# A decoder layer on one core: rotary halves exchanged by DMA, three-pass attention scores, top-4 by match and replace

## Chip, cores and metric

One core of one Trainium2 chip runs the whole layer in one launch. The metric is the device time of a launch in microseconds (us): lower is better. The median of three runs of the kernel before is 417.92 us (417.89 to 418.08).

## What is computed

Four sequences (`B`=4) of 256 tokens with 256 channels pass through one layer: self-attention, cross-attention and a block-sparse feed-forward network, each followed by a residual sum and a layer norm. Cut to what the change touches:

```python
# self-attention: 16 query heads, 2 key/value heads of 128
qkv = hidden_states @ Wqkv
x1, x2 = (x[..., :D // 2], x[..., D // 2:])            # rotary embedding of q and k
out = jnp.concatenate([x1 * cos - x2 * sin, x1 * sin + x2 * cos], axis=-1)
logits = jnp.einsum('bqhd,bkhd->bhqk', xq, xk) * SCALE
logits = SOFTCAP * jnp.tanh(logits / SOFTCAP)          # then causal mask, softmax, @ xv, @ Wo
# feed-forward router: the 4 most probable of 16 blocks of 64 hidden units
prob = jax.nn.softmax(xf @ Wr.T + br, axis=-1)
_, idx = jax.lax.top_k(prob, TOP_K)
mask = mask.at[jnp.arange(n)[:, None], idx].set(1.0)
h = jax.nn.gelu(h, approximate=False) * mask[:, :, None]
```

## The kernel before

Work is cut into operations `(kind, b, i, t)`: a kind, a sequence b, an index i (a head pair, a quad of heads, a half of the network) and, for the parts that go by token tile, the tile t of 128 tokens. Each engine runs its own share of every operation, in one common order, `plan`. `plan` is built from the string `ORDER`: each letter takes the next operation of one stream (`r` rotary projections, `s` scores, `m` probabilities times values and the output projection, `c` context, `x` and `y` cross-attention of tile 0 and 1, `n` and `o` the network of tile 0 and 1). So an engine whose next instruction waits holds up all that stands behind it in `plan`, on that engine alone; engines meet through semaphores. SP, the queue that issues nearly all DMAs, walks the same `plan`. PSUM has seven rotating banks (`claim`), and an eighth for the sum of the output projection (`acc`).

The parts that the change touches:

- `rot(b, i)`: PE projects one pair of heads (i=0 is the keys), 24 matmuls of 256 columns in three passes over parts of the operands (high times high, high times low, low times high: `three_pass`, L438). DVE's `rope` multiplies the bank by cosine (L928) and, each half of the partitions apart, the exchanged halves by sine (L931, L932) into `rope_t`. POOL's `rotate` adds the two (L1223) into `q_T` or `k_T`. `q_T` has four pair slots.
- `near(b, j)` and `far(b, i)`: PE multiplies keys and queries in plain fp32, 512 columns in one matmul (L469, L477). ACT applies tanh and exp (L773, L775), POOL the causal selection (L1241). `mix` on PE (L492, L495) then needs what POOL selected.
- `turn(b, j)`: PE transposes a pair's output; ACT takes it out of PSUM twice, rounded into `a_hi` and as it is into `a_flat`; POOL subtracts (L1234, `a_lo`); `proj` on PE (L525) needs `a_lo`.
- `wo`: ACT rounds (L791) and POOL takes the rest (L1229) of a weight slot, for the first sequence alone; later ones reload the parts (`wo_s<-wo_parts`).
- `route(b, t)`: DVE turns 16 probabilities into a mask of 4 by comparing each with each: L1125, L1126, L1130, L1132, L1134, then L1137. `turn_m`, the masked half of `hidden` and `ffn` on PE wait for it.
- `turn_q`: ACT copies transposed queries into `qS`, two quads of heads deep for each tile.

Of the kernel before, what the change touches and what calls it, by code (L numbers as in the profile page):

```python
# [65 lines left out]
def rotate_ops(b):  # L66
# [8 lines left out]
    return [(kind, b, i, 0) for kind, i in ops]  # L75

# [46 lines left out]
def network_ops(b, t):  # L123
# [12 lines left out]
    "rrrrrrrrrmmsrssrrmmsmrmssmrmmrrmmmsscmmmsmmmmmmccmmsssmmmcccmmmmrrmmmmccmmmrmmrrmsssmccmmmrmmsssmmmyrmmmx"  # L136
    "rsmssxyrmmmxmsmymrmmxsmysxxmmmmyrrymymmmxxxxysyryrmmrmyxyyxxxxyyxyxmmxyyxxymmmxmssxrrxyyxysxmymyyssxmmmmy"
    "xxccmmmsrsrnsmmmmsxyrcmcccmmymmsmsyxmrmmmxnmmmmmxxmnymrrnnyxxxxyyrxxxxmyxyyxxxxmyyxmmoxyyyxroyyxyymssxyym"
    "xosryyxroxysymysmmxmmsyccnoxymycomcomyccxsymnssrymxmymxxymyrxsxxmyxxyxxyyxyyyoymmxxyxxyxyymxyxxnyyxsxxsym"
    "yyxmmmmoxynmmmmmycmmcmmmmnxyccccooxnxyynxyxxyoyoxyyyyxyyxyyonxyyyxxxxyxxxyxyxxyyxxnyxyxyoxooyynnxnxnnnooo"  # L140
    "nnnoonoo")


# [24 lines left out]
PER = {"x_hi": 1, "x_lo": 1, "roped": 3 * (PAIRS + 1), "rotated": PAIRS + 1, "values": 1,  # L168
# [9 lines left out]
def build_decoder(nc, x, xT, ctxT, mask, wqkv, wo, wkvT, xwq, xwo, xbias, wrT, br, w1T, w2T,  # L178
# [10 lines left out]
    with ExitStack() as ctx:  # L189
# [42 lines left out]
        a_flat = sb("a_flat", [2, 2, T])  # L232
# [1083 lines left out]
```

## Time and profile before

| | |
|---|---|
| median of three runs | 417.92 us (417.89 to 418.08) |
| profiled execution, its own time | 418.27 us |
| its span, first to last instruction | 416.5 us |
| PE busy | 383.6 us, 92% |
| DVE busy | 345.8 us, 83% |
| ACT busy | 248.2 us, 60% |
| POOL busy | 151.3 us, 36% |
| granted TensorE clock | 0.999 of full speed |

Busy times are those of the page. A busy PE is one with a matmul in its pipeline, and PE's instructions overlap: a 256-column matmul is shown with 0.28 us though the next one starts after 0.12 us. Costs of PE are therefore read from distances between starts.

### The profile page before, as it was taken

What the parts mean: (1) busy time and instruction counts of PE and PEld (TensorE: products, weight loads), DVE (VectorE), ACT (ScalarE), POOL (GpSimd) and SP (SyncE); (2) the same over time, 40 slices, a digit from 0 to 9 for tenths busy, and PEclk for the clock granted to TensorE, in tenths of its full rate; (3) what the DMA queues carried; (4) which work ended last, traced back from release to release, by engine and by line L of the source; (5) the groups of instructions that cost most, each with busy time, mean ns of one, the idle gap of its engine ahead of it and who ended that gap; (6) DMA issues with size and microseconds to landing.
All of it is one profiled execution on the core that took longest, in us unless ns stands there. A gap on an engine that the chain in (4) does not pass through costs nothing.

```text
span 416.5 us, 9192 instructions
## 1 busy us (share of the span) xinstructions
PE 383.6 (92%) x3144; PEld 327.9 (79%) x3144; DVE 345.8 (83%) x967; ACT 248.2 (60%) x528; POOL 151.3 (36%) x174
## 2 busy tenths in 40 slices
PE   2889999999999999999999999999889989889895
PEld 2868779887799877788998686978768977668784
DVE  4999987589989679889997998888798887888753
ACT  5266543545777775365689665389974247984230
POOL 7488636745544233455331133143113221000101
PEclk9999999999999999999999999999999999999999
DMA  6993342511311230213303000121103000000000
GB/s 213 334 344 127 124 144 89 182 48 51 102 50 53 84 121 2 76 58 105 121 1 102 2 27 27 39 65 51 52 27 103 2 0 14 15 2 0 14 15 25
DMA packets 16814, 31.36 MB, mean 75 GB/s; under 512 B 1665, under 2 KB 10753, under 8 KB 16769
## 3 DMA queue, kind: packets, MB, share of 16 engines
q1 hardware_dynamic: 15952, 29.98, 21.8%
q10 hardware_dynamic: 816, 0.79, 0.7%
q8 instruction: 27, 0.44, 0.4%
q14 instruction: 19, 0.15, 0.1%
HBM read 25.52 MB, written 5.24 MB: 74 GB/s over the span
## 4 chain that ended last, share of the span: by engine, by line
PE 48%; DVE 30%; issue 9%; ACT 6%; POOL 3%; DMA 3%; SPq 0%; DVEq 0%; POOLq 0%; ACTq 0%
PE bank L438 10%; PE acc L525 7%; PE bank L611 4%; PE bank L492 4%; PE bank L663 3%; PE bank L469 3%; PE bank L600 3%; ACT xs L817 2%; PE bank L506 2%; PE bank L623 2%; DMA xs<-in_wo 2%; PE bank L477 2%; DVE rope_t L932 2%; DVE rope_t L931 2%; PE bank L678 2%
## 5 line engine op out<-in xcount | busy, mean ns | idle before, releaser
L1223 POOL TENSOR_TENSOR q_T<-q_T,rope_t 128x512 f32<-128x512 f32 x32 | 43.0, 1345 | 45.0 <-DVE rope_t L932 45.0
L817 ACT ACTIVATE xs<-xs,xneg 128x256 f32<-128x256 f32 x128 | 54.5, 502 | 6.6 <-DVE xneg L1069 6.4
L1234 POOL TENSOR_TENSOR a_lo<-a_flat,a_hi 128x512 fp32r<-128x512 f32 x32 | 41.9, 1310 | 38.6 <-ACT a_flat L738 38.6
L438 PE MATMUL bank<-x_hi,wqkv_hi 128*128 128x256 f32 x144 | 45.6, 317 | 8.8 <-DVE wqkv_lo L904 8.8
L1252 POOL TENSOR_TENSOR rstd<-var_eps,half 128x1 f32<-128x1 f32 x24 | 13.2, 552 | 108.0 <-DVE var_eps L956 108.0
L525 PE MATMUL acc<-wo_s,a_hi 128*128 128x256 f32 x256 | 50.4, 295 | 0.9 <-POOL a_lo L1234 0.9
L1069 DVE CUSTOM_DVE_ANT_0 xs<-bank,mask_s 128x256 f32<-128x256 f32 x128 | 46.0, 418 | 0.6 <-PE bank L600 0.6
L492 PE MATMUL bank<-v_s,p_near 128*128 128x129 f32 x256 | 42.5, 278 | 1.2 <-POOL p_far L1241 0.8
L525 PEld LDWEIGHTS acc<-wo_s,a_hi 128*128 128x128 f32 x256 | 39.5, 189 | 3.8 <-issue 2.1
L492 PEld LDWEIGHTS bank<-v_s,p_near 128*128 128x128 f32 x256 | 35.8, 191 | 8.4 <-issue 6.6
L438 PE MATMUL bank<-x_lo,wqkv_hi 128*128 128x256 f32 x144 | 41.7, 289 | 0.0
L438 PE MATMUL bank<-x_hi,wqkv_lo 128*128 128x256 f32 x144 | 41.6, 289 | 0.0
L611 PE MATMUL bank<-ident_s,xs 128*128 128x128 f32 x256 | 36.2, 277 | 1.2 <-ACT xs L817 0.4
L438 PEld LDWEIGHTS bank<-x_hi,wqkv_hi 128*128 128x128 f32 x144 | 28.5, 198 | 10.5 <-issue 10.0
L525 PE MATMUL acc<-wo_s,a_lo 128*128 128x256 f32 x128 | 35.9, 280 | 0.0
L773 ACT ACTIVATE p_near<-bank 128x512 f32<-128x512 f32 x32 | 19.1, 596 | 26.7 <-PE bank L469 26.5
L738 ACT CAST a_hi<-bank 128x512 fp32r<-128x512 f32 x32 | 18.9, 591 | 24.3 <-PE bank L506 23.7
L611 PEld LDWEIGHTS bank<-ident_s,xs 128*128 128x128 f32 x256 | 28.4, 141 | 6.3 <-issue 3.4
L469 PE MATMUL bank<-q_T,k_T 128*128 128x512 f32 x64 | 32.3, 598 | 0.1
L663 PE MATMUL bank<-z_T,w_s 128*128 128x128 f32 x256 | 31.8, 277 | 0.5 <-DVE stage L1144 0.5
L663 PEld LDWEIGHTS bank<-z_T,w_s 128*128 128x128 f32 x256 | 30.0, 192 | 0.8 <-DVE stage L1144 0.7
L678 PE MATMUL bank<-w_s,stage 128*128 128x256 f32 x128 | 29.2, 381 | 0.5 <-DVE stage L1144 0.5
(150 smaller groups left out, 976.2 us busy)
## 6 DMA issues: line engine op xcount, KB each, us to landing
wo_s<-wo_parts SPq DMA_DIRECT2D x24, 512.0 KB, 3.3
wo_parts<-wo_s SPq DMA_DIRECT2D x8, 512.0 KB, 2.9
stage<-in_wqkv SPq DMA_DIRECT2D x5, 512.0 KB, 4.3
xs<-in_wo SPq DMA_DIRECT2D x8, 256.0 KB, 4.3
y<-in_x SPq DMA_DIRECT2D x4, 256.0 KB, 2.7
ctx_s<-in_ctxT SPq DMA_DIRECT2D x4, 256.0 KB, 4.7
mask_s<-in_mask SPq DMA_DIRECT2D x4, 256.0 KB, 2.7
w_s<-in_w1T SPq DMA_DIRECT2D x1, 1024.0 KB, 11.3
```

Of the source, the lines that this page charges most:

```text
L438: ins = mm(ps, lhs[i], rhs[j], start=(k == 0 and n == 0), stop=(last and n == 2))
L469: mm(ps[:, :], k_T[:, j // 4, 0:P], q_T[:, j % 4].rearrange("p h q -> p (h q)"), start=True, stop=True).then_inc(filled, 1)
L492: ins = mm(o, p_near[:, j % NEAR, m, t * P:(t + 1) * P], v_s[:, 0, j // 4, :], start=True, stop=(t == 0))
L525: ins = mm(acc[:, t, :], a[x], wo_s[:, slot, w, m, :], start=(j == 0 and t == 0 and m == 0 and p == 0), stop=(j == PAIRS - 1 and m == 1 an ...
L611: ins = transpose(ps[:, m2 * T + k * P:m2 * T + (k + 1) * P], xs[:, t, m, m2, k * P:(k + 1) * P], ident_s[:])
L663: ins = mm(ps[:, m * P:(m + 1) * P], w1_s[:, k, (n * part + m) * P:(n * part + m + 1) * P], z_T[:, t, k, :], start=(k == 0), stop=(k == CK ...
L678: ins = mm(ps[:, 0:C], g_T[:, t, n, :], w2_s[:, n, :], start=(n == 0), stop=(n == HT - 1))
L773: activation(dst, bank(kind, b, i)[:], ACT.Tanh, scale=SCALE / SOFTCAP).then_inc(sig["capped", 0], 1)
L817: activation(xs[:, t, m, m2, :], xs[:, t, m, m2, :], ACT.Exp, bias=xneg[:, t, m, m2:m2 + 1], scale=-1.0)\
L1069: do(v.tensor_tensor_reduce(out=xs[:, t, m, m2, :], in0=bank("xscore", b, g, t, m)[:, m2 * T:(m2 + 1) * T], in1=mask_s[:, t, :], scale=-1. ...
L1223: g.tensor_tensor(dst, dst, rope_t[:, n % 2], ALU.add).then_inc(sig["rotated", 0], 1)
L1234: g.tensor_tensor(a_lo[:, j % 2], a_flat[:, j % 2], a_hi[:, j % 2].bitcast(F32), ALU.subtract)\
```

## The change

Five edits. The rotary result is rounded on ACT into a high part (`q_hi`, `k_hi`), and POOL takes the rest (`q_lo`, `k_lo`), a new operation `round` with the letter `q` in `ORDER`; the scores become three passes of 512 columns. From the second sequence on DVE multiplies by sine over all 128 partitions, and two DMAs exchange the halves into `rope_s`; POOL adds after they have landed. The router takes DVE's eight largest values, marks four of them by `match_replace`, and compares. `a_flat` and `qS` have one buffer where they had two, `ones` lies inside `xs`, and the DMA scratch is smaller. `ORDER` is a new string, of 569 letters after 533.

```diff
-    "rrrrrrrrrmmsrssrrmmsmrmssmrmmrrmmmsscmmmsmmmmmmccmmsssmmmcccmmmmrrmmmmccmmmrmmrrmsssmccmmmrmmsssmmmyrmmmx"
+    "rrrrrqrqmmrrqrmqrsssqrrsmmqmrssmmmmqsrmmmmmqssrmmmmcrmqmmsmccmmmmssrrmcmmmqqmcrmcmmmmsqmmrrmmmsqqmccmsrrm"
...
-        a_flat = sb("a_flat", [2, 2, T])
+        a_flat = sb("a_flat", [2, T])
-        qS = sb("qS", [TT, 2, 2, 2, P], F32R)
+        qS = sb("qS", [TT, 2, 2, P], F32R)
...
+            def swap_halves(b, i):
+
+                n = b * (PAIRS + 1) + i
+                lower, upper = slice(0, HD // 2), slice(HD // 2, HD)
+                if n >= 2:
+                    sp.wait_ge(sig["rotated", 0], n - 1)
+                wait_for(sp, "roped", b, 3 * i)
+                for dst, src in ((lower, upper), (upper, lower)):
+                    sp.dma_start(rope_s[dst, n % 2], rope_t[src, n % 2]).then_inc(swapped[n % 2], 16)
...
             def near(b, j):
...
-                wait_for(pe, "rotated", b, j + 1)
-                mm(ps[:, :], k_T[:, j // 4, 0:P], q_T[:, j % 4].rearrange("p h q -> p (h q)"),
-                   start=True, stop=True).then_inc(filled, 1)
+                wait_for(pe, "q_lo", b, j + 1)
+                three_pass(ps[:, :], [a[:, j // 4, 0:P] for a in (k_hi, k_lo)],
+                           [a[:, j % 4].rearrange("p h q -> p (h q)") for a in (q_hi, q_lo)], 0, True).then_inc(filled, 1)
...
+            def rounding(b, i):
+
+                if i == 0:
+                    wait_filled(act, "far", b - 1, QUADS - 1)
+                else:
+                    j = i - 1
+                    wait_filled(act, "far", *((b, (j - 4) // 2) if j >= 4 else (b - 1, (j + PAIRS - 4) // 2)))
+                wait_for(act, "rotated", b, i)
+                copy(rotary(i)[0], rope_c[:, (b * (PAIRS + 1) + i) % 2]).then_inc(sig["q_hi", 0], 1)
...
+                evacuate(a_hi[:, j % 2].rearrange("p h q -> p (h q)"), bank("turn", b, j)[:], "turn", b, j, 0, "attn_T")
+                if j or b:
+                    wait_for(act, "attn_lo", *divmod(b * PAIRS + j - 1, PAIRS))
+                evacuate(a_flat[:].rearrange("p h q -> p (h q)"), bank("turn", b, j)[:], "turn", b, j, 0, "attn_T")
...
-                wait_filled(act, "xscore", *((b, g - 2) if g >= 2 else (b - 1, g + QUADS - 2)), t, 1)
+                wait_filled(act, "xscore", *((b, g - 1) if g else (b - 1, QUADS - 1)), t, 1)
...
                 if n >= 2:
-                    dve.wait_ge(sig["rotated", 0], n - 1)
...
+                    dve.wait_ge(sig["q_lo", 0], n - 1)
+                dst = rope_c[:, n % 2]
...
+                if b:
+                    if n >= PAIRS + 3:
+                        dve.wait_ge(swapped[n % 2], 32 * swaps_before(n))
+                    v.tensor_tensor(rope_t[:, n % 2], ps, s, ALU.mult).then_inc(sig["roped", 0], 1)
+                    v.tensor_tensor(dst, ps, c, ALU.mult).then_inc(sig["roped", 0], 2)
+                    return
...
-                do(v.tensor_tensor(above[:, t], other, own, ALU.is_gt))
-                do(v.tensor_tensor(equal[:, t], other, own, ALU.is_equal))
+                do(v.max(best[:, t, 8 - TOPK:16 - TOPK], prob[:, t, :]))
...
-                do(v.tensor_tensor(equal[:, t], equal[:, t], before_s[:], ALU.mult))
-                done()
-                do(v.tensor_tensor(above[:, t], above[:, t], equal[:, t], ALU.add))
-                done()
-                do(v.tensor_reduce(rank[:, t, :], above[:, t], AX_X, ALU.add))
+                do(v.match_replace(marked[:, t, :], best[:, t, 0:8], prob[:, t, :], -1.0))
...
                 wait_for(pool, "roped", b, 3 * i + 2)
-                g.tensor_tensor(dst, dst, rope_t[:, n % 2], ALU.add).then_inc(sig["rotated", 0], 1)
+                if b:
+                    pool.wait_ge(swapped[n % 2], 32 * (swaps_before(n) + 1))
+                g.tensor_tensor(dst, dst, (rope_s if b else rope_t)[:, n % 2], ALU.add).then_inc(sig["rotated", 0], 1)
+
+            def rounding(b, i):
+
+                hi, lo = rotary(i)
+                wait_for(pool, "q_hi", b, i)
+                g.tensor_tensor(lo, rope_c[:, (b * (PAIRS + 1) + i) % 2], hi.bitcast(F32), ALU.subtract).then_inc(sig["q_lo", 0], 1)
```

What the new string does is seen in each engine's order. POOL's queue at the start of the first sequence, right behind the constants, was (`q_T<-q_T,rope_t` is a `rotate`, `wo_s` the rest of an output weight, `p_near` and `p_far` causal selections):

```order
L1223 TENSOR_TENSOR k_T<-k_T,rope_t 128x512
L1223 TENSOR_TENSOR q_T<-q_T,rope_t 128x512 x3
L1229 TENSOR_TENSOR wo_s<-xs,wo_s 128x512
L1241 AFFINE_SELECT p_near<-p_near 128x2x128
L1223 TENSOR_TENSOR q_T<-q_T,rope_t 128x512
L1241 AFFINE_SELECT p_near<-p_near 128x2x128
L1241 AFFINE_SELECT p_far<-p_far 128x512
L1223 TENSOR_TENSOR q_T<-q_T,rope_t 128x512
```

And now (`rope_c` is the rotary sum, `k_lo` and `q_lo` the new rests):

```order
L1256 TENSOR_TENSOR rope_c<-rope_c,rope_t 128x512 x2
L1262 TENSOR_TENSOR k_lo<-rope_c,k_hi 128x512
L1262 TENSOR_TENSOR q_lo<-rope_c,q_hi 128x512
L1268 TENSOR_TENSOR wo_s<-xs,wo_s 128x512
L1256 TENSOR_TENSOR rope_c<-rope_c,rope_t 128x512 x2
L1262 TENSOR_TENSOR q_lo<-rope_c,q_hi 128x512
L1268 TENSOR_TENSOR wo_s<-xs,wo_s 128x512
L1262 TENSOR_TENSOR q_lo<-rope_c,q_hi 128x512
L1256 TENSOR_TENSOR rope_c<-rope_c,rope_t 128x512
L1280 AFFINE_SELECT p_near<-p_near 128x2x128 x2
L1280 AFFINE_SELECT p_far<-p_far 128x512
L1262 TENSOR_TENSOR q_lo<-rope_c,q_hi 128x512
```

Each rotation now has a second POOL instruction some places behind it, and the third and fourth rotation have moved behind the first output weight.

DVE's queue in a router of the last sequence was:

```order
L1119 RECIPROCAL r_rec<-r_sum 128x1
L1121 TENSOR_SCALAR prob<-prob,r_rec 128x16
L1125 TENSOR_TENSOR above<-prob 128x256
L1126 TENSOR_TENSOR equal<-prob 128x256
L1130 TENSOR_TENSOR equal<-equal,before_s 128x256
L1132 TENSOR_TENSOR above<-above,equal 128x256
L1134 TENSOR_REDUCE rank<-above 128x16
L1137 TENSOR_SCALAR keep<-rank 128x16
```

And now:

```order
L1158 RECIPROCAL r_rec<-r_sum 128x1
L1160 TENSOR_SCALAR prob<-prob,r_rec 128x16
L1162 MAX best<-prob 128x8
L1166 MATCH_REPLACE marked<-best,prob 128x16
L1169 TENSOR_SCALAR keep<-marked 128x16
```

Two instructions on 16 values stand where five stood on 256.

SP's queue from the last stores of the first sequence to the second sequence's first reload of output weights (`L391` is `swap_halves`, two DMAs a rotation) is now:

```order
L380 DMA wo_parts<-wo_s 128x1024
L391 DMA rope_s<-rope_t 64x512 x4
L367 DMA xs<-in_wo 128x2x256
L380 DMA wo_parts<-wo_s 128x1024
L391 DMA rope_s<-rope_t 64x512 x2
L367 DMA xs<-in_wo 128x2x256
L395 DMA ctx_s<-in_ctxT 128x2x256
L380 DMA wo_parts<-wo_s 128x1024
L375 DMA wo_s<-wo_parts 128x1024
L391 DMA rope_s<-rope_t 64x512 x4
```

Before, the same stretch had the same loads and stores without the rows of L391: 54 such DMAs are new in the whole program.

## Rows read from the trace of the kernel before

**Rows 1.** Window, length, busy PE, PEld, DVE, ACT, POOL, granted clock, DMA share, GB/s

```profile
12.00:66.00 54.00, 50.49 (x340) 41.65 (x339) 50.31 (x92) 27.77 (x50) 34.07 (x33) 1.00 0.59 201
66.00:120.00 54.00, 52.36 (x383) 45.46 (x382) 42.78 (x103) 31.74 (x63) 32.45 (x35) 1.00 0.30 98
120.00:200.00 80.00, 77.66 (x672) 66.89 (x672) 68.33 (x190) 48.95 (x107) 33.40 (x37) 1.00 0.21 67
200.00:300.00 100.00, 96.73 (x855) 82.57 (x854) 88.41 (x281) 74.87 (x166) 28.33 (x33) 1.00 0.16 49
300.00:392.00 92.00, 82.88 (x752) 69.92 (x753) 77.15 (x258) 54.54 (x128) 13.97 (x18) 1.00 0.06 19
392.00:417.00 25.00, 18.85 (x132) 16.79 (x130) 12.36 (x39) 5.03 (x10) 1.65 (x3) 0.98 0.07 22
```

**Rows 2.** What PE waited for: us in total, times, longest

```profile
PE bank L438 <- DVE wqkv_lo L904: 8.8, 2, 7.4
PE bank L623 <- DVE xp_T L1078: 4.3, 6, 0.9
```

**Rows 3.** The chain that ended last, by engine (the page)

```profile
PE 48%; DVE 30%; issue 9%; ACT 6%; POOL 3%; DMA 3%; SPq 0%; DVEq 0%; POOLq 0%; ACTq 0%
```

**Rows 4.** PE in order of time: start, us shown, instruction

```profile
18.59 0.28 PE L438 MATMUL bank<-wqkv_lo,x_hi 128*128 128x256 f32 x1
18.71 0.28 PE L438 MATMUL bank<-wqkv_hi,x_lo 128*128 128x256 f32 x1
...
21.10 1.02 PE L469 MATMUL bank<-q_T,k_T 128*128 128x512 f32 x2
21.96 1.02 PE L477 MATMUL bank<-q_T,k_T 128*128 128x512 f32 x2
```

**Rows 5.** DVE's groups by form: busy us and mean ns, idle before

```profile
L931 DVE TENSOR_TENSOR rope_t<-bank,sin_s 64x512 f32<-64x512 f32 x36 | 25.0, 693 | 1.1
L932 DVE TENSOR_TENSOR rope_t<-bank,sin_s 64x512 f32<-64x512 f32 x36 | 24.6, 684 | 1.1
L928 DVE TENSOR_TENSOR q_T<-bank,cos_s 128x512 f32<-128x512 f32 x32 | 21.9, 686 | 5.1 <-PE bank L438 4.8
L1121 DVE TENSOR_SCALAR prob<-prob,r_rec 128x16 f32<-128x16 f32 x8 | 2.0, 255 | 0.3
```

**Rows 6.** The chain in the last stretch: start, us, what

```profile
398.44 0.42 DVE above L1125
...
399.89 0.43 DVE rank L1134
```

**Rows 7.** Groups of POOL and ACT by form, as in rows 5

```profile
L1223 POOL TENSOR_TENSOR q_T<-q_T,rope_t 128x512 f32<-128x512 f32 x32 | 43.0, 1345 | 45.0 <-DVE rope_t L932 45.0
L1234 POOL TENSOR_TENSOR a_lo<-a_flat,a_hi 128x512 fp32r<-128x512 f32 x32 | 41.9, 1310 | 38.6 <-ACT a_flat L738 38.6
L1241 POOL TENSOR_SCALAR_AFFINE_SELECT p_near<-p_near 128x256 f32<-128x256 f32 x32 | 14.2, 447 | 30.5 <-ACT p_near L775 30.4
L1229 POOL TENSOR_TENSOR wo_s<-xs,wo_s 128x512 fp32r<-128x512 f32 x8 | 11.2, 1404 | 9.4 <-ACT wo_s L791 9.4
L1241 POOL TENSOR_SCALAR_AFFINE_SELECT p_far<-p_far 128x512 f32<-128x512 f32 x16 | 10.4, 648 | 10.9 <-ACT p_far L775 10.9
L751 ACT CAST x_hi<-xT_s 128x512 fp32r<-128x512 f32 x4 | 2.5, 616 | 2.0 <-DMA xT_s<-in_xT 1.6 <-PE bank L438 0.4
```

**Rows 8.** POOL in order of time, idle before in brackets

```profile
12.63 1.29 POOL L1223 TENSOR_TENSOR k_T<-k_T,rope_t 128x512 f32<-128x512 f32 x1 [4.42 <-DVE rope_t L932]
15.12 1.79 POOL L1223 TENSOR_TENSOR q_T<-q_T,rope_t 128x512 f32<-128x512 f32 x1 [1.19 <-DVE rope_t L932]
```

**Rows 9.** DMAs: SP's issue of a 128 KB store, its landing; a larger reload

```profile
L420 SPq DMA_DIRECT2D out_y<-stage x8: 332/335/357, 264.3 to 414.4; - x8
DMA to landing us min/median/max: 1.7/1.7/2.0
wo_s<-wo_parts SPq DMA_DIRECT2D x24, 512.0 KB, 3.3
```

**Rows 10.** One DVE line: ns min/median/max of ten

```profile
L904 DVE TENSOR_TENSOR wqkv_lo<-stage,wqkv_hi x10: 677/1100/1780, 5.8 to 28.9; 128x512 fp32r<-128x512 f32 x10
```

More of the change, by code:

```diff
@@ L75, in rotate_ops, with round_ops @@
     return [(kind, b, i, 0) for kind, i in ops]
+def round_ops(b):
+    return [("round", b, i, 0) for i in range(PAIRS + 1)]
 def score_ops(b):
@@ L163, in make_plan @@
     return plan
[L168 removed]
+PER = {"x_hi": 1, "x_lo": 1, "roped": 3 * (PAIRS + 1), "rotated": PAIRS + 1, "q_hi": PAIRS + 1, "q_lo": PAIRS + 1, "values": 1,
        "capped": PAIRS + QUADS, "expd": PAIRS + QUADS, "causal": PAIRS + QUADS, "attn_rec": NH,
@@ L222, in build_decoder @@
         x_hi, x_lo = sb("x_hi", [CK, T], F32R), sb("x_lo", [CK, T], F32R)
-        rope_t = sb("rope_t", [2, 2, T])
-        q_T = sb("q_T", [4, 2, T])
-        k_T = sb("k_T", [NKV, T])
+        rope_t, rope_c, rope_s = (sb(name, [2, 2, T]) for name in ("rope_t", "rope_c", "rope_s"))
+        q_hi, q_lo = sb("q_hi", [4, 2, T], F32R), sb("q_lo", [4, 2, T], F32R)
+        k_hi, k_lo = sb("k_hi", [NKV, T], F32R), sb("k_lo", [NKV, T], F32R)
         v_s = sb("v_s", [TT, NKV, HD + 1])
@@ L287, in build_decoder @@
         wo_hi, wo_lo = sem("wo_hi"), sem("wo_lo")
+        swapped = [sem(f"swapped{i}") for i in range(2)]
         piece_hi, piece_lo = sem("piece_hi"), sem("piece_lo")
@@ L303, in bank, with rotary, swaps_before @@
             return banks[where[kind, b, i, t, k] % NBANK]
+        def rotary(i):
+            pair = (k_hi[:], k_lo[:]) if i == 0 else (q_hi[:, (i - 1) % 4], q_lo[:, (i - 1) % 4])
+            return pair
+        def swaps_before(n):
+            return len(range(PAIRS + 1 + (n - PAIRS - 1) % 2, n, 2))
         def wait_filled(eng, kind, b, i=0, t=0, k=0):
@@ L405, in _ @@
                 both = all((kind, b, i, n) in done for n in range(TT))
-                if kind == "quant_w" and i == 1:
+                if kind == "rot" and b:
+                    swap_halves(b, i)
+                elif kind == "quant_w" and i == 1:
                     load_tokens(1)
@@ L542, in turn_w @@
                 for o in range(CK):
-                    ins = mm(ps[:, o * P:(o + 1) * P], ones[:], q_tmp[:, o, 0:P], start=True, stop=True)
+                    ins = mm(ps[:, o * P:(o + 1) * P], ones, q_tmp[:, o, 0:P], start=True, stop=True)
                 ins.then_inc(filled, 1)
@@ L845, in _ @@
                     val(b)
+                elif kind == "round":
+                    rounding(b, i)
                 elif kind in ("near", "far"):
@@ L1233, in rest_attn @@
                 wait_for(pool, "attn_T", b, 2 * j + 1)
-                g.tensor_tensor(a_lo[:, j % 2], a_flat[:, j % 2], a_hi[:, j % 2].bitcast(F32), ALU.subtract)\
+                g.tensor_tensor(a_lo[:, j % 2], a_flat[:], a_hi[:, j % 2].bitcast(F32), ALU.subtract)\
                     .then_inc(sig["attn_lo", 0], 1)
@@ L1258, in _ @@
                     rotate(b, i)
+                elif kind == "round":
+                    rounding(b, i)
                 elif kind == "wo":
```

62 lines of the change are left out of this document (24 added, 38 removed).

## Prediction

> **What bounds the kernel now.** I read the busy times in stretches first, to see which engine is full where; then what PE waited for; then the chain that ended last. In the stretches [rows 1] PE is busy 50.5 of 54 us, 52.4 of 54, 77.7 of 80, 96.7 of 100: from 12 to 300 us it stands idle for 10.8 us of 288, under 4%. After 300 us it is looser: 9.1 us idle of 92, and 5.7 us between 392 us and the end at 416.5. No wait of PE is large but the start, where it waits for the first weights to be split (8.8 us in two waits, 7.4 of them before its first matmul); the next in the list, for DVE's `xp_T`, is 4.3 us in six pieces [rows 2]. The chain goes 48% through PE and 30% through DVE [rows 3], so DVE, busy 50.3 of 54 us in the first stretch and 88.4 of 100 in the fourth [rows 1], is a near second. POOL is full nowhere: at most 34.1 of 54 us, in the first stretch [rows 1]. So I count first what PE's own work loses, and then look where other engines' waits could reach PE.
>
> **Scores on PE.** A score matmul of 512 columns in fp32 is two records, and from the start of one to the start of the next score passes 21.96 − 21.10 = 0.86 us [rows 4]. A pass of the three-pass kind on 256 columns passes in 18.71 − 18.59 = 0.12 us [rows 4]. No such pass of 512 columns is in this trace. From above it is two of 256, 0.24, so three are 0.72 us. From below, the fp32 score taken as four passes makes 0.215 a pass, and three are 0.645 us. I take the middle, 0.68, since a wider matmul pays its fixed part once: 0.18 us less for each of 48 scores (12 in each of four sequences), 8.6 us; the bounds are 48 × 0.14 = 6.7 and 48 × 0.215 = 10.3. This is PE's own time in stretches in which it is over 95% busy, so it should come off the end.
>
> The Trainium skill (FP8 and Floating Point Precision, "TensorE Precision Notes") says that true FP32 takes four passes through the array; the two records of 0.43 us fit this as two passes each, and by the page alone a score would fall to three quarters, 0.645 us, which is the bound from below and 10.3 us in all.
>
> **Rotary products on DVE.** In sequences 1 to 3, 27 rotations lose one of their three products, which take 0.69, 0.68 and 0.69 us [rows 5] whether on 64 or 128 partitions: 27 × 0.69 = 18.6 us of DVE. In the first sequence nothing is saved.
>
> **Router on DVE.** From the start of L1125 to the end of L1134 pass 399.89 + 0.43 − 398.44 = 1.88 us [rows 6]. For the two new instructions the nearest row on 16 values is a product of 0.255 us [rows 5]; two such, with a short wait between them, are 0.55. From below they could not be less than nothing, which adds 0.55 a router. From above, each could take 0.43, as L1134 does on 256 values [rows 6]: 0.9. I take 0.55, so 1.3 us less for each of eight routers, 10.6 us of DVE. DVE's load falls by 29 us in all. In the last stretch two routers lie in the chain one behind the other, so up to 2.7 us could come off; PE's own 18.9 of 24.5 us there [rows 1] leave 5.7 us of idle, part of it behind the last matmul, so I take 2.0.
>
> DVE's relief elsewhere: between 300 and 392 us PE idles 9.1 us [rows 1], in part for DVE. Four routers fall there, which gives DVE back 5.3 us. I take a quarter of that as seen by PE, 1.3 us; the bounds are 0 and, were DVE behind all of it, 5.3.
>
> **Rounding on ACT and POOL.** 36 rotations each gain a cast of 0.62 us on ACT (22 us, from 248 of 416 us) and a subtraction on POOL like L1234, 1.31 us (47 us, from 151) [rows 7]. Both engines have the room in the sum; the question is the queue. In the first sequence a rotation waits for the `q_lo` of the last but one. I followed POOL's new order from 12.6 us [rows 8] with 1.3 us for each sum and rest, 0.45 and 0.65 for selections, 1.4 for an output weight [rows 7]: the second `rotate` starts at 15.1 [rows 8], the two rests end at about 19.5, the first weight at 20.9, rotations three and four at about 25, and the third rest at about 26.4. PE starts at 7.4 [rows 2]; three rotations and the values (each 24 passes of 0.12, 2.9 us) are done at 18.9 and two more rotations at 24.6; it does the first score and stands before the second at 25.3: a wait of 1.1 us. Against that, the values now stand ahead of the third rotation and cover PE's other wait for split weights, 8.8 − 7.4 = 1.4 us [rows 2]. From there POOL is nearly full up to 65 us: 34.1 us of work in that stretch before [rows 1], and eleven rests of 1.31 more, 48 of 54 us. Small stalls of PE in front of `mix`, `near` and `proj` will come of this; net I book +1.5 us for the start (bounds 0 and 5).
>
> **The exchange by DMA.** SP takes 0.34 us to issue a DMA, and 128 KB land after 1.7 us [rows 9]. The two of a rotation land about 0.34 + 0.34 + 1.7 = 2.4 us after `rope_t`, that is 0.69 + 2.4 = 3.1 us after DVE began, where the third product ended at 2.1: POOL's sum starts 1.0 us later. Behind a reload of 512 KB, which alone takes 3.3 us [rows 9], it may be 2 more. While POOL stands at the sum, the rests for `proj`, the selections for `mix` and the powers that the layer norms wait for stand behind it. The cover is PE's own rotation, 2.9 us, and that POOL idled 45 us for the same release already [rows 7]. A rotation and its rounding now pass in 0.69 + 2.4 + 1.3 + 0.6 + 1.3 = 6.3 us with two in flight, 3.2 us each, against PE's 2.9, and only where rotations stand back to back. I book +2.0 us for 27 rotations (bounds 0 and 8). SP waits at an exchange for `rope_t`; the reloads behind it come in the same order as before, with three slots of lead, and I book nothing; without that lead a reload that lands late would cost `proj` its 3.3 us.
>
> **The rest, at nothing.** `turn_q` with one `qS` waits for a score that stands ahead of it on PE, so it is over when the transposed queries arrive. The second copy into `a_flat` waits for POOL's last rest; where POOL is punctual, a `proj` of twelve passes, 1.4 us, lies between. Uncovered it would be up to 1.3 us each. ACT loads a table of functions ten times where it was twelve; ACT is not full, and this covers part of the new casts. `ones` and the scratch move nothing that an engine executes.
>
> **Sum.** 416.5 − 8.6 − 2.0 − 1.3 + 1.5 + 2.0 = 408.1 of span. The execution's own time is 1.8 us above its span and 0.35 above the median, so 408.1 + 1.4 = 409.5 us on the scale of the medians, 8.4 below 417.92, or 2.0%.
>
> **Rivals.**
> *DVE was the holder.* DVE is 79 to 93% busy in the stretches up to 392 us and 30% of the chain [rows 1, 3]. If most of PE's small waits were its doing, its 29 us of relief would also take half of the 20 us that PE idles between 12 and 392: 409.5 − 8 = 401.5. Against it: PE's listed waits for DVE are few [rows 2].
> *POOL becomes the bound at the start.* If each of the first nine `q_lo` reached PE half a microsecond late beyond what I booked, and `proj` likewise, the start costs its upper bound of 5 us and 2 more: 415. For it, 48 of 54 us of POOL's time filled; against it, PE itself was busy 50.5 of the same 54 [rows 1], more than POOL will be.
> *POOL stands before the exchange, and PE behind it: slower.* If the exchange's 1.0 us is seen by PE in each of 27 rotations at 0.4 us or more, on top of the bound of 5 at the start, this is 10.8 + 5 − 3.5 already booked = 12.3 more: 421.8. It decides from about 8.4/27 = 0.31 us a rotation beyond what I booked. For it: POOL executes in plan order, and its queue also carries the layer norms' powers; SP's queue stands in front of exchanges behind 512 KB reloads. Against it: POOL is busy a third of the time after 66 us [rows 1].
> *POOL and DVE in each other's way.* L904, two SBUF inputs, took 0.68 us at best and 1.10 in the median [rows 10], and POOL's sum beside it took 1.79 where it takes 1.29 [rows 8]. Each of 36 new subtractions that meets such a DVE instruction so costs 0.5 us on either side; if half meet, 9 us of each engine, which the 29 us of relief swallow. All 36, each seen by PE for a third, would be 6 us: 415.5. The Trainium skill (SBUF — State Buffer, "SBUF: two separate sides") has DVE with two SBUF inputs and a reading GpSimd exclude each other for a whole instruction. By it a meeting would cost up to 1.3 us, 36 × 1.3 = 47 us of DVE in the worst case, more than the relief; the row's 0.5 us is far less than that.
> *The transfer is no faster.* That the rotary edit brings nothing in time is already my forecast: its relief is not on PE.
>
> **Chances.** My own case, 405 to 413: 0.60. DVE's relief counts, below 405: 0.13. POOL at the start or the two engines in each other's way, 413 to 417: 0.13. The slower case, over 418: 0.11. The rest, within 0.2% of 417.92, which is about what this kernel's measurement can tell: 0.03. Faster by over 0.2%: 0.84; within 0.2%: 0.04; slower: 0.12. The range that leaves out 2 in 10 runs from 402 to 417.
>
> **What the next profile would show.** Scores: three records a score, 0.645 to 0.72 us from first to next; otherwise the first term is mis-sized. DVE busy near 317 us; far above, the engines are in each other's way (L904's new line tells it). PE's busy time 375 us. PE's waits between 20 and 60 us for `q_lo`, `p_near` or `a_lo` of at most 3 us together. POOL's waits for `rope_s` DMAs, with PE waiting for POOL in sequences 1 to 3 hardly at all. If PE's idle time between 66 and 300 us rises from 7.2 to over 15, the prediction is wrong by the exchange.

## The result: 3.3% slower

The changed kernel takes 431.31 us in the median of four runs (430.09 to 432.67), where the kernel before, run beside it on the same chip, takes 417.9. The ratio is 1.0325, 95% interval 1.029 to 1.0359: 13.4 us slower. The forecast was 409.5 us, and faster; it lies 22 us off, and the range missed as well. Ratios are of undisturbed executions alone: one of a_warm's four (632.2 us, mean granted clock 0.56) and one of the kernel beside it (484.06 us, 0.76) are left out. The profiled execution took 430.29 us, its span is 428.5.

The page after: busy times, the share of PE's clock in tenths by slice, and the shares of the chain that ended last.

```profile
span 428.5 us, 9480 instructions
PE 383.0 (89%) x3192; PEld 340.7 (79%) x3192; DVE 325.2 (76%) x924; ACT 263.1 (61%) x562; POOL 196.1 (46%) x209
...
PEclk9989969999999999999999998999999999999999
...
PE 49%; DVE 18%; POOL 9%; issue 9%; ACT 6%; DMA 6%; SPq 2%; POOLq 0%; DVEq 0%; ACTq 0%
```

DVE's share of the chain fell from 30% to 18% [rows 3], as its relief would let one expect. But POOL, the DMAs and SP's queue now hold 17% together, where POOL and DMAs held 6%, and the end came later. The same stretches as in [rows 1]:

```profile
core 0: us, PE busy (x) PEld busy (x) DVE busy (x) ACT busy (x) POOL busy (x), PEclk, DMA share, GB/s
12.00:66.00 54.00, 44.01 (x295) 40.19 (x294) 43.67 (x78) 32.36 (x58) 44.90 (x41) 0.91 0.55 189
66.00:120.00 54.00, 50.64 (x374) 45.08 (x372) 34.81 (x77) 28.24 (x53) 40.40 (x40) 1.00 0.45 132
120.00:200.00 80.00, 74.47 (x656) 66.26 (x657) 62.80 (x179) 55.27 (x123) 43.45 (x43) 1.00 0.33 93
200.00:300.00 100.00, 93.86 (x799) 84.03 (x799) 83.62 (x243) 66.91 (x145) 45.32 (x47) 0.98 0.27 75
```

From 12 to 300 us PE stands idle for 25.0 us (288 − 263.0), where it was 10.8. The first stretch gives 6.5 of these 14.2 us, at a mean clock of 0.91; the later ones give the rest. POOL is busy 44.9 of 54 us in the first. The waits after, PE's own and the largest of POOL and ACT around the rotary:

```profile
engine line waited for: us in total, times, longest us
POOL rope_c L1256 <- DMA rope_s<-rope_t: 53.6, 19, 6.5
ACT q_hi L786 <- POOL rope_c L1256: 28.8, 14, 6.2
POOL a_lo L1273 <- ACT a_flat L763: 26.3, 15, 4.7
...
PE bank L463 <- DVE wqkv_lo L943: 8.9, 2, 7.4
PE bank L463 <- POOL q_lo L1262: 5.6, 2, 4.9
PE bank L636 <- ACT xs L854: 3.3, 4, 1.9
```

Only 5.6 us of PE's waits bear the name of `q_lo`. The remaining loss has no large wait of its own: it is spread over many small gaps. So the list alone doesn't explain the result. The timeline of PE at the first scores, and of POOL beside it:

```profile
19.84 0.40 PE L463 MATMUL bank<-q_hi,k_hi 128*128 128x512 f32 x1
20.08 0.40 PE L463 MATMUL bank<-q_lo,k_hi 128*128 128x512 f32 x1
20.31 0.40 PE L463 MATMUL bank<-q_hi,k_lo 128*128 128x512 f32 x1
25.58 0.77 PE L463 MATMUL bank<-q_hi,k_hi 128*128 128x512 f32 x1 [4.87 <-POOL q_lo L1262]
26.14 0.63 PE L463 MATMUL bank<-q_lo,k_hi 128*128 128x512 f32 x1
26.57 0.63 PE L463 MATMUL bank<-q_hi,k_lo 128*128 128x512 f32 x1
26.99 0.63 PE L463 MATMUL bank<-q_hi,k_hi 128*128 128x512 f32 x1
```

```profile
20.56 1.27 POOL L1256 TENSOR_TENSOR rope_c<-rope_c,rope_t 128x512 f32<-128x512 f32 x1
22.49 1.27 POOL L1256 TENSOR_TENSOR rope_c<-rope_c,rope_t 128x512 f32<-128x512 f32 x1 [0.65 <-DVE rope_t L971]
23.71 1.73 POOL L1262 TENSOR_TENSOR q_lo<-rope_c,q_hi 128x512 fp32r<-128x512 f32 x1
25.40 1.73 POOL L1268 TENSOR_TENSOR wo_s<-xs,wo_s 128x512 fp32r<-128x512 f32 x1
```

A pass of 512 columns passes in 20.31 − 20.08 = 0.23 us. The second score needs the rest that POOL begins at 23.71, behind two sums, and PE stands 4.87 us for it. After that wait a pass takes 26.57 − 26.14 = 0.43 us, nearly twice as long: the clock has gone from 2.4 to 1.2 GHz, and stays there 3.4 us.

POOL's costliest groups, and SP's rows at exchanges between 80 and 102 us:

```profile
L1262 POOL TENSOR_TENSOR q_lo<-rope_c,q_hi 128x512 fp32r<-128x512 f32 x32 | 43.4, 1366 | 4.5 <-ACT q_hi L786 4.5
L1256 POOL TENSOR_TENSOR rope_c<-rope_c,rope_s 128x512 f32<-128x512 f32 x27 | 35.0, 1297 | 53.9 <-DMA rope_s<-rope_t 53.6
```

```profile
L391 SPq DMA_DIRECT2D rope_s<-rope_t x8: 462/568/597, 84.0 to 99.6; - x8
...
DMA to landing us min/median/max: 2.2/2.8/5.3
```

From the start of DVE's first rotary product to the start of POOL's sum now pass 4.5, 3.7 and 4.1 us on average in sequences 1, 2 and 3, where it was 2.2 to 2.8. From the end of a rotation on PE until its operand is ready pass 12.5, 12.5 and 10.7 us; before, it was 5.3, 4.4 and 4.4. In sequence 0, where nothing is exchanged, 5.4 became 8.8. These are means that I worked out from the starts and ends of the instructions of each rotation. For sequence 1 the same count gives 7.1 us without the rounding (a_fp32 below) and 9.1 with the rounding but without POOL's rests (a_norest).

### The profile page after: what moved, and what is told of

Its sections match the earlier page's. It is cut to its first block, busy times and chain, and to the rows that moved or that the text cites. A ratio compares the mean times of both kernels' runs of the same rounds, so it can differ in the third digit from the quotient of the medians.

```text
span 428.5 us, 9480 instructions
## 1 busy us (share of the span) xinstructions
PE 383.0 (89%) x3192; PEld 340.7 (79%) x3192; DVE 325.2 (76%) x924; ACT 263.1 (61%) x562; POOL 196.1 (46%) x209
## 3 DMA queue, kind: packets, MB, share of 16 engines
q1 hardware_dynamic: 20272, 37.06, 28.5%
## 4 chain that ended last, share of the span: by engine, by line
PE 49%; DVE 18%; POOL 9%; issue 9%; ACT 6%; DMA 6%; SPq 2%; POOLq 0%; DVEq 0%; ACTq 0%
PE bank L463 12%; PE bank L636 5%; PE acc L550 5%; PE bank L703 5%; PE bank L688 5%; DMA rope_s<-rope_t 4%; POOL rope_c L1256 3%; PE bank L517 3%; PE bank L625 3%; PE bank L648 2%; ACT xs L854 2%; POOL q_lo L1262 2%; PE bank L531 2%; PE bank L520 2%; POOL rstd L1291 1%
## 5 line engine op out<-in xcount | busy, mean ns | idle before, releaser
L1256 POOL TENSOR_TENSOR rope_c<-rope_c,rope_s 128x512 f32<-128x512 f32 x27 | 35.0, 1297 | 53.9 <-DMA rope_s<-rope_t 53.6
L463 PE MATMUL bank<-x_hi,wqkv_hi 128*128 128x256 f32 x144 | 43.2, 300 | 9.0 <-DVE wqkv_lo L943 8.9
L550 PE MATMUL acc<-wo_s,a_hi 128*128 128x256 f32 x256 | 48.7, 289 | 1.5 <-POOL a_lo L1273 1.3
L1262 POOL TENSOR_TENSOR q_lo<-rope_c,q_hi 128x512 fp32r<-128x512 f32 x32 | 43.4, 1366 | 4.5 <-ACT q_hi L786 4.5
L636 PE MATMUL bank<-ident_s,xs 128*128 128x128 f32 x256 | 37.2, 282 | 3.5 <-ACT xs L854 3.3
L786 ACT CAST q_hi<-rope_c 128x512 fp32r<-128x512 f32 x32 | 19.6, 620 | 30.7 <-POOL rope_c L1256 28.8
L463 PEld LDWEIGHTS bank<-x_hi,wqkv_hi 128*128 128x128 f32 x144 | 28.2, 196 | 10.3 <-issue 9.9
L1117 DVE COPY xp_T<-bank 128x512 f32<-128x512 f32 x32 | 22.0, 687 | 11.8 <-PE bank L636 11.7
L763 ACT CAST a_hi<-bank 128x512 fp32r<-128x512 f32 x32 | 18.7, 584 | 19.5 <-PE bank L531 19.1
```

The lines of the kernel that those rows point to most:

```text
L463: ins = mm(ps, lhs[i], rhs[j], start=(k == 0 and n == 0), stop=(last and n == 2))
L550: ins = mm(acc[:, t, :], a[x], wo_s[:, slot, w, m, :], start=(j == 0 and t == 0 and m == 0 and p == 0), stop=(j == PAIRS - 1 and m == 1 an ...
L636: ins = transpose(ps[:, m2 * T + k * P:m2 * T + (k + 1) * P], xs[:, t, m, m2, k * P:(k + 1) * P], ident_s[:])
L1117: v.tensor_copy(xp_T[:, t, 1].rearrange("p m k q -> p (m k q)"), bank("turn_p", b, i, t)[:])\
L1256: g.tensor_tensor(dst, dst, (rope_s if b else rope_t)[:, n % 2], ALU.add).then_inc(sig["rotated", 0], 1)
L1262: g.tensor_tensor(lo, rope_c[:, (b * (PAIRS + 1) + i) % 2], hi.bitcast(F32), ALU.subtract).then_inc(sig["q_lo", 0], 1)
```

## The experiments

Two letters stand in the names. Runs a_… have the new `ORDER` (a_start a rearranged one), runs bo_… the changed code with the old `ORDER`, into which the letter `q` is put three operations behind each rotation; where there is no rounding, `q` does nothing. b_router is the kernel before with one edit. The kernel before took 417.6 to 418.1 us in each call.

### One part at a time

**b_router**: the kernel before with the new router alone.

```diff
-                do(v.tensor_tensor(above[:, t], other, own, ALU.is_gt))
-                do(v.tensor_tensor(equal[:, t], other, own, ALU.is_equal))
...
+                do(v.max(best[:, t, 8 - TOPK:16 - TOPK], prob[:, t, :]))
...
```

> The kernel before with the new router alone (eight largest, match and replace), its own order and all else. From the trace the two new instructions take 0.43 us where five took 1.88: about 1.4 us less for each of eight routers. If two of them are seen in the tail, as predicted, 415 (2 to 3 us less than 417.9); if PE hides them, 417 to 418.

Measured: 414.10 us, ratio 0.9911 (0.9894 to 0.9927): 3.95 us off the 418.05 beside it. My terms for the router, 2.0 + 1.3, were close in sum.

**a_noswap, a_fp32, a_neither**: the changed kernel without the exchange, without the rounding, without both.

```diff
-                if b:
...
-                    v.tensor_tensor(rope_t[:, n % 2], ps, s, ALU.mult).then_inc(sig["roped", 0], 1)
-                    v.tensor_tensor(dst, ps, c, ALU.mult).then_inc(sig["roped", 0], 2)
-                    return
...
-                three_pass(ps[:, :], [a[:, j // 4, 0:P] for a in (k_hi, k_lo)],
...
+                mm(ps[:, :], k_T[:, j // 4, 0:P], q_T[:, j % 4].rearrange("p h q -> p (h q)"),
```

> The changed kernel without the exchange: in all four sequences DVE makes three products and POOL adds as soon as they are there, no DMA of rope_s. All else, the order too, as changed (431.3 us). Theory S (the loss is made at the start, where POOL's queue of sums, rests and weights keeps the second score waiting and PE's clock then falls): nothing changes before 66 us, and the time stays within 2 us of 431. Theory X (the loss comes from POOL standing 53.6 us before the landing of exchanges in sequences 1 to 3): about 7 us come back, 424. Theory D (DVE is the real second bound): 27 third products, 18.6 us, come back onto DVE, and the time rises above 433.

> The changed kernel with scores in plain fp32: no rounding on ACT, no rest on POOL, one fp32 matmul a score; the exchange, the router, the buffers and the order (round operations left out) as changed. Theory S: the wait of 4.9 us before the second score and both falls of the clock before 66 us go; scores cost 48 x 0.16 = 7.7 us more; 431.3 - 11 + 7.7 = about 428. Theory X: nothing comes back, 431 to 439.

> The changed kernel with neither the exchange nor the three-pass scores: what is left of the change is the new order (round operations left out), the router and the single buffers. If the order by itself suits the old work, 413 to 418, near the kernel before less the router's gain. If the order is part of the loss, over 420. With the other two runs this gives the exchange's cost without rounding (a_fp32 less this) and the rounding's without exchange (a_noswap less this).

Measured: a_noswap 440.58 us, 1.0547 (1.0523 to 1.0572); a_fp32 419.94, 1.004 (1.0022 to 1.0057); a_neither 430.22, 1.0297 (1.0281 to 1.0313). So in the new order the exchange saves 9.3 us with rounding (440.6 to 431.3) and 10.3 without (430.2 to 419.9), and the rounding costs 11.4 us with exchange and 10.4 without. The exchange, which I had booked as a loss, is the only part besides the router that helps. And with neither, the kernel is 12 us slower than before: something that the forecast had no term for. Of the expectations, the third of a_noswap (DVE is a second bound) and the second of a_neither (the order is part of the loss) came true; both of a_fp32 missed, the nearer by 8 us.

**bo_neither, bo_swap, bo_round, bo_all**: the same four with the old order.

> The changed kernel's code with the order of the kernel before, without exchange and without rounding: against b_router (414.1) only a_flat, qS and ones have less room; against a_neither (430.2) only the order differs. Theory O (the new order itself costs the old work 16 us): 414 to 416. Theory B (the single buffers cost it): 425 to 430.

> As bo_neither, with the exchange by DMA in sequences 1 to 3. On the new order the exchange took off 10.3 us (430.2 to 419.9). Theory D (DVE is a bound in any order, and 18.6 us of relief count): 5 to 10 us below bo_neither, 405 to 410. Theory X (the exchange helps only an order made for it; in the old one POOL stands before the landing): above bo_neither, 416 to 422.

> As bo_neither, with the rounding and the three-pass scores, a round operation set three operations behind its rotation in the old order. On the new order the rounding cost 10.4 us (430.2 to 440.6). If it is the start that costs (POOL's queue, then the clock), the same here, for POOL is as full: 422 to 428. If it was the new order's place for it, 408 to 416, by the 7.7 us that the scores lose on PE.

> All of the change, but the old order with round operations three operations behind their rotations. If the parts add as on the new order: bo_neither - 10.3 + 11.4, about 416. Theory O then has the new order cost 15 us of the changed kernel (431.3 less this). If the new order is needed by the new work, this is above 431.

| | old order | new order |
|---|---|---|
| neither | 414.26, 0.9922 (0.9904 to 0.994) | 430.22 |
| exchange | 425.48, 1.0188 (1.0172 to 1.0205) | 419.94 |
| rounding | 447.76, 1.0724 (1.0701 to 1.0747) | 440.58 |
| both | 480.01, 1.1495 (1.1463 to 1.1527) | 431.31 |

bo_neither is as fast as b_router: the single buffers of `a_flat` and `qS` cost nothing, as forecast. The new order costs the old work 16.0 us, but saves 48.7 us once both edits are there. The edits and the order can't be priced apart. The expectations for bo_neither and bo_all came true in one of their branches; bo_swap and bo_round came out slower than either of theirs, bo_round by 20 us. In the old order the waits of PE do bear POOL's name. First bo_swap's, then bo_round's, then bo_all's:

```profile
PE acc L549 <- POOL a_lo L1259: 5.9, 3, 4.5
PE bank L493 <- POOL q_T L1248: 4.8, 2, 2.4
```
```profile
PE bank L461 <- POOL q_lo L1252: 15.1, 7, 4.4
```
```profile
PE bank L463 <- POOL q_lo L1262: 17.0, 5, 4.7
PE acc L550 <- POOL a_lo L1273: 7.1, 3, 4.5
```

PE's mean clock is 0.94 in bo_all's profile, against 0.983 in the changed kernel's, so a part of bo_all's excess may be the clock's; how large a part, no run tells.

### Where the rounding's cost sits

**a_start32**: fp32 scores without rounding in sequence 0 alone. **a_warm**: 30 matmuls whose results nobody reads, 18 in PE's wait before the second score and 12 before the first weight transpose at some 55 us. **a_start**: the new order with two pieces at the start rearranged, so that a rotation's rest stands further ahead of its score.

```diff
+                if (b, j) == (0, 1):
+                    warm(ps, 18)
```
```diff
-    rrrrrqrqmmrrqrmqrsssqrrsmmqmr
+    rrrrrqrqmrqrqrmrsssmqrrsmmqmr
...
-    smccmmmmssrrmcmmmqqmcr
+    smmmmmssrrccmmcmmqqmcr
```

> The changed kernel with plain fp32 scores and no rounding in the first sequence alone; three passes in the others, exchange, order as changed. Theory S: the 11.4 us that the rounding costs (a_fp32 419.9 against 431.3) lie at the start, so nearly all come back: 419 to 423. If they lie in all sequences alike, a quarter: 427 to 430.

> The changed kernel with idle PE filled: 18 extra matmuls of 512 columns (0.23 us each, 4.2 us) into the second score's own bank before its wait, and 12 more (2.8 us) before the first weight transpose (turn_w). They compute nothing that is read. The waits stay; only PE's clock should no longer fall. Theory K (the two falls before 66 us, 10.2 us of half clock, cost half their length): 431.3 - 5 = 426. If other engines held the pace then anyway, no change, 430 to 432; if the extra work delays the score, up to 433.

> The changed kernel with two places of its order mended: the first two output weights stand behind the rests of the third and fourth rotation, which frees q_lo for the second score 1.3 us and more earlier, and turn_w with quant_w of the second weight stand behind the first two rotations of sequence 1. Theory S: waits of 4.9 and 2.9 us shrink to 2 to 3 and 0, the clock stays up or falls once less: 424 to 428. If PE only waits elsewhere instead, 430 to 432.

Measured: a_start32 429.28 us, 1.0254 (1.0208 to 1.0299); a_warm 429.38 (three executions), 1.0262 (1.0219 to 1.0305); a_start 439.20, 1.0513 (1.0484 to 1.0543). By the ratios, 1.0325 less 1.0254, the rounding in sequence 0 costs about 3 us of the 13, up to 5 by the two intervals: no more than a quarter of the rounding's 11.4 and some noise, as one expects if all sequences pay alike. In a_warm the clock stays up from 20 to 34 us, and this gives some 2 us, within the spread of the two kernels' executions (427.4 to 430.1 against 430.1 to 432.7):

```profile
20.00:34.00 14.00, 12.33 (x71) 10.11 (x70) 12.38 (x17) 9.47 (x17) 13.36 (x12) 1.00 0.89 321
```

a_start, meant to mend the start, made the kernel 8 us slower, outside both of its expectations.

**a_late**: from the second sequence on, POOL runs a sum that waits for an exchange up to four of its own operations later, so that rests and selections can pass it. **a_noswap3, a_fp32_3, bo_swap3**: three rotary buffers instead of two.

> The changed kernel with POOL's order alone altered: from the second sequence on each sum of the rotary parts stands up to four of POOL's operations later, so that what stood behind the wait for the exchange (53.6 us in 19 waits) goes first. Theory X (POOL's standing before the landing is what the rest of the change pays for): 431.3 - 3 to 6 = 425 to 428. If the rounding behind the sum is what PE needs most, its delay costs as much: 431 to 435.

> a_noswap (changed, exchange undone, 440.6) with three buffers for the rotary products where it had two, so that DVE's next rotation waits for the rest of the last but two. Theory L (the rounding costs by its loop: product, sum, cast, rest, next product, with two in flight): 4 to 10 us come back, 431 to 437. Theory Q (it costs by POOL's queue and room alone, 45 us more of work in plan order): no change, 439 to 442.

> a_fp32 (changed, fp32 scores without rounding, 419.9) with three rotary buffers. Theory L for the exchange (product, DMA, sum, next product, two in flight): 2 to 5 us come back, 415 to 418. If POOL's standing before the landing is the cost, whatever the buffers: 419 to 421.

> bo_swap (order of the kernel before, new router, exchange, fp32 scores, 425.5) with three rotary buffers. The old order has rotations closer together, so theory L gives most here: 414 to 419, and below 414 if the relief of DVE then shows. If POOL's standing is the cost: 424 to 426.

Measured: a_late 451.87 us, 1.0818 (1.0787 to 1.0848). This is 17 us beyond either expectation. ACT needs the sum for its cast, and its wait for it grew from 28.8 to 57.0 us:

```profile
ACT q_hi L787 <- POOL rope_c L1257: 57.0, 22, 5.6
```

The third buffer changes nothing: 440.89, 419.86 and 425.43 us against 440.58, 419.94 and 425.48 with two. So two rotations in flight are not too few.

**a_norest, bo_round_norest**: everything as in the changed kernel, and as in bo_round, but POOL's 36 rests are left out; the low parts are zero. PE still makes three passes and ACT still casts. **a_restdve**: DVE computes the rests.

```diff
-                wait_for(pool, "q_hi", b, i)
-                g.tensor_tensor(lo, rope_c[:, (b * (PAIRS + 1) + i) % 2], hi.bitcast(F32), ALU.subtract).then_inc(sig["q_lo", 0], 1)
...
-                wait_for(pe, "q_lo", b, j + 1)
+                wait_for(pe, "q_hi", b, j + 1)
```

> The changed kernel without POOL's 36 rests: q_lo and k_lo are set to zero once at the start, PE's three passes and DVE's rotary wait for ACT's cast alone. It leaves out the low part of queries and keys (the low products are made with zeros). All else, the order too, is the changed kernel's. Theory Q (the rest's 1.3 us in POOL's queue is what rounding costs, since sums, rests and selections stand one behind the other there): the time falls from 431.3 to 420 or below, 8 of the 11.4 us that fp32 scores gave back, plus the 8 us that the passes save, so as low as 412. Rival R (ACT's cast and the longer chain of handovers are the cost, or the order itself): 427 or above, at most 4 us back. Between 420 and 427 both have a part.

> The kernel with the old order, no exchange, three-pass scores (447.8 us before), without POOL's 36 rests as above (low parts are zero). Theory Q: 414.3 less the scores' 8, plus little, so 408 to 420. Rival R: 435 or above, since the chain from DVE through POOL's sum to ACT's cast still stands in front of the scores.

> The changed kernel with the 36 rests computed on DVE instead of POOL, at the same letters of the order. DVE's instruction should take about 0.7 us instead of 1.3, and POOL loses 47 us of work, but DVE now stands in front of the cast, which waits for the sum and the exchange. Theory Q: if POOL's queue is the price, below 428. Rival R: DVE's own wait for the cast puts more behind it than POOL's queue loses: 433 or above.

Measured: a_norest 416.34 us, 0.996 (0.9936 to 0.9984); bo_round_norest 425.56, 1.0185 (1.017 to 1.02); a_restdve 455.50, 1.0896 (1.0859 to 1.0934). The 36 rests alone cost 15.0 us in the new order and 22.2 in the old. a_norest fits the theory that the rest on POOL is the price; bo_round_norest, at 425.6, lies between its two (408 to 420, or 435 and above). The waits of a_restdve and the windows and groups of a_norest show how:

```profile
POOL rope_c L1264 <- DMA rope_s<-rope_t: 69.1, 18, 8.2
...
DVE q_lo L977 <- ACT q_hi L786: 25.5, 16, 3.9
```

```profile
12.00:66.00 54.00, 45.79 (x331) 41.78 (x331) 45.56 (x84) 32.84 (x59) 32.78 (x32) 0.97 0.58 195
66.00:120.00 54.00, 52.85 (x401) 48.81 (x401) 37.63 (x96) 34.56 (x67) 32.19 (x35) 1.00 0.47 138
120.00:200.00 80.00, 78.02 (x696) 70.32 (x696) 62.23 (x183) 53.93 (x120) 32.64 (x36) 1.00 0.36 103
```

```profile
L1068 DVE TENSOR_TENSOR parts<-parts 128x512 fp32r<-128x512 f32 x8 | 6.0, 754 | 0.3
L1098 DVE TENSOR_TENSOR parts<-q_tmp,parts 128x512 fp32r<-128x512 f32 x8 | 5.5, 692 | 0.3
```

and the same two groups in the changed kernel:

```profile
L1066 DVE TENSOR_TENSOR parts<-parts 128x512 fp32r<-128x512 f32 x8 | 8.8, 1105 | 0.3
L1096 DVE TENSOR_TENSOR parts<-q_tmp,parts 128x512 fp32r<-128x512 f32 x8 | 7.4, 931 | 0.3
```

Without the rests POOL is busy 32.8 us instead of 44.9 in the first stretch, PE 78.0 instead of 74.5 in the third, and a rotation's operand is ready 9.1 us after PE's end in sequence 1, not 12.5. DVE is busy 313.7 us in all, not 325.2: the 36 rests cost DVE 11.5 us, 0.32 each. About 8.2 us of this lie in groups whose two inputs are in SBUF, as the two above; but groups with one such input grew too (`q_tmp<-q_tmp`, 256 columns, from 394 to 498 ns each). On DVE the rest does away with POOL's share, but DVE then stands 25.5 us before it for ACT's cast, with the rotary products, the normalisations and the masks behind it, and the kernel is 24 us slower still; its mean clock is 0.967, lower than the changed kernel's. The theory that had expected a gain from that move missed. The rest was free on neither of the two engines that were tried; that this is for the work behind it in the queue is what the waits suggest, not what a run isolates.

## Why the prediction was wrong

The steps from before to after, each a difference of two medians: router −3.9 us (418.05 to 414.10), single buffers 0 (414.26), the new order with the old work +16.0 (430.22), the exchange −10.3 (419.94), rounding with three passes but without POOL's rests −3.6 (416.34), POOL's rests +15.0 (431.31). They were measured in this sequence, and by the table above another sequence would give other prices. My sum had −3.3, 0, nothing, +2.0, −8.6 + 1.5 for both last steps together.

**The term for scores on PE was right as PE's work and wrong as time.** Three passes take 3 × 0.23 = 0.69 us where I took 0.68. For 48 scores PE's work falls by 48 × (0.86 − 0.69) = 8.2 us (8.6 forecast). "This is PE's own time in stretches in which it is over 95% busy, so it should come off the end": this step failed. A full PE was taken to stay full, and its operands to come no later. Without POOL's rests only 3.6 of the 8.2 arrive, and with them the rounding is 11.4 us on the wrong side.

**"Both engines have the room in the sum; the question is the queue"** named the right question and answered it too small. I booked 1.5 us, bounds 0 to 5, and looked only at the start. The rounding's share there is some 3 us (a_start32), but POOL's rests cost 15 over the whole kernel. The traces show two things that the rests do. First, the latency of a rotation more than doubled. In the kernel before, one operand in each of the sequences 0 to 2 was ready only 0.1 to 0.8 us ahead of its score; there was no slack to spend, and a share of busy time of 36% doesn't show that. Second, POOL and DVE disturb each other: 11.5 us of DVE's time. This rival put 9 us on DVE if half of the rests meet such an instruction, so as engine time it was near; whether the 6 us that it gave PE were right, no run shows. The Trainium skill (SBUF — State Buffer, "SBUF: two separate sides") has the one wait for the other's whole instruction, by estimate up to 36 × 1.3 = 47 us if every rest met one. In the trace 12 of the 36 rests overlap a DVE instruction with two inputs in SBUF; they take 1.53 us on average and the others 1.30, and 8.2 us of DVE's time over 12 meetings is 0.7 us each, about half an instruction of POOL.

**The start was walked with a wrong count.** I took a rotation as 24 passes, 2.9 us, as the description of `rot` ahead of the prediction also has it; the trace has 12 (1.42 us). It misplaced PE by 4.6 us at the second score, so 4.87 us of wait stand where I had 1.1, and it also made "3.2 us each, against PE's 2.9" look balanced, when a rotation on PE takes 1.4 us. The number of instructions in the page's group, x144 a kind for 36 rotations (three kinds, so 12 each), would have told it.

**The exchange: the terms were too small, the sign was wrong.** SP takes 0.46 to 0.60 us an issue here and up to 1.17 elsewhere, not 0.34; the landing takes 2.2 to 5.3 us, not 1.7. POOL's sum starts 1.5 to 1.9 us later than in the kernel before, where I had 1.0. Yet in the new order it saves 10 us, because DVE loses 19.5 us of work (334.6 to 315.1 busy from a_neither to a_fp32; 18.6 forecast). I had set the worth of DVE's relief there at nothing; the rival "DVE was the holder" was right in this one link, for the new order. In the old order the same exchange costs 11.2 us, 0.42 us for each of 27 rotations, and PE's two waits for POOL shown above make 10.7 us, where a wait for `a_lo` took 0.9 before. That is the rival "POOL stands before the exchange, and PE behind it" with its 0.4 us a rotation, but in an order that it was not made for, so its nearness is luck. I read the two results as the order leaving, or not leaving, 2 us more between a rotation and what needs it; no run isolates this.

**The order had no term.** I read the changed plan only for POOL's first steps. That it costs the old work 16 us was not looked for. In a_neither the time is lost in all stages: with every matmul counted at its undisturbed distance, PE loses, against bo_neither, about 4 us more from 12 to 66 us, under 1 up to 120, 5 up to 200, 2 up to 300 and 4 after. Which of its moves cost this stays open; only one rearrangement was tried (a_start, worse).

**The clock.** I booked nothing. In the changed kernel PE runs at 1.2 GHz for 13.7 us in three pieces before the end, which can add at most half of that, 6.8 us. a_warm has 10.3 us less of such time, worth at most 5.1, and got back some 2, so part of it was probably covered by waits that would have come anyway.

**The signs that I had named.** DVE is busy 325.2 us where I wrote near 317, and that did point at POOL and DVE in each other's way. PE is busy 383.0 us where I wrote 375. PE's idle time between 66 and 300 us rose from 7.2 to 15.0 us, just at the sign that should have meant "wrong by the exchange"; but without the exchange (a_noswap) the kernel is 9.3 us slower, so this sign pointed at the wrong part.

What stays open: how the 15.0 us of the rests divide between the queue and the disturbance of DVE. a_restdve took the rests out of POOL's queue but put a worse wait into DVE's; a rest on an engine with nothing behind it was not tried. a_norest also lets DVE's next rotation and PE's score go after ACT's cast, so its 15.0 us hold that shorter loop as well. In the old order the rounding costs 11.3 us even without the rests (414.26 to 425.56), though PE has 8 us less to do. The cast in ACT's queue and the rotary products that wait for it are what is left there, and no run tells them apart.

## What to carry to other kernels

Work that lies "in the idle half" of an in-order engine was not free here, where results pass through it on their way to the bound engine: count the latency from producer to consumer and compare it with the slack of the tightest consumer, not with the engine's idle share. Price an order written by hand with the work it was made for: the same two edits were worth +66 us in one order and +1 in the other. And count instructions from the page's groups before walking a timeline.

The fastest version measured is the kernel before with the new router alone, 414.10 us; nothing else in this change improved on it.

## What the hardware showed

- PE's clock fell to 1.2 GHz in a wait of 4.87 us (25.1 to 28.5 us), with two short ones close together, 1.67 and 1.18 us (55.8 to 62.7), and after one of 1.87 (264.0 to 267.5). The length of a wait alone doesn't tell: PE's wait of 2.17 us before 122.0 brought no fall in the changed kernel, and the same wait, 2.18 us, brought one in a_warm (121.9 to 125.3). With the first two places filled, a_warm stayed at full clock through both. In the kernel before, no wait behind the first matmul (the longest 1.37 us) brought a fall before the end. The changed kernel's rows, and a_warm's row last:

```profile
24.00:28.00 4.00, 2.42 (x6) 1.99 (x7) 3.94 (x5) 2.42 (x6) 4.00 (x3) 0.64 1.05 370
...
56.00:60.00 4.00, 3.35 (x15) 3.38 (x16) 3.86 (x12) 0.71 (x2) 1.69 (x3) 0.50 0.13 45
60.00:64.00 4.00, 4.00 (x19) 3.58 (x19) 3.09 (x11) 2.38 (x5) 1.30 (x2) 0.67 0.27 69
124.00:128.00 4.00, 4.00 (x31) 3.74 (x30) 3.79 (x14) 3.09 (x7) 1.27 (x2) 1.00 0.01 2
264.00:268.00 4.00, 4.00 (x15) 3.26 (x16) 3.20 (x8) 2.55 (x8) 1.73 (x2) 0.57 0.19 59
...
122.00:126.00 4.00, 4.00 (x18) 3.54 (x18) 2.74 (x9) 0.79 (x3) 0.00 (x0) 0.58 0.00 0
```

- The two router instructions that replace five are three records in the trace. Near the end 1.88 us [rows 6] became 411.54 + 0.16 − 411.25 = 0.45 us, and the one that finds the eight largest of 16 values takes 0.18 us, as long as the comparison behind it (0.17).

```profile
411.25 0.18 DVE L1162 MAX8 best<-prob 128x8 f32<-128x16 f32 x1
411.46 0.09 DVE L1166 MATCH_VALUE_LOAD marked<-best,prob 128x8 f32 x1
411.54 0.16 DVE L1166 MATCH_REPLACE8 marked<-best,prob 128x16 f32<-128x16 f32 x1
411.73 0.17 DVE L1169 TENSOR_SCALAR keep<-marked 128x16 bf16<-128x16 f32 x1
```

- An exchange of partitions within SBUF by DMA, 128 KB, lands no earlier than 2.2 us after its issue, where a store of 128 KB landed after 1.7 [rows 9].
